# One block for the convolutions and the attention, and a single last tile

## The reference, cut to what matters

```
h = layernorm(conv2(gelu(conv1(x))) + x)            # grouped convolutions over 5 tokens, 4 hidden channels a channel
for i in range(4):                                  # linear attention with 16 heads
    q = gelu(h @ Wq[i] + bq[i]) + 0.21;  k = gelu(h @ Wk[i] + bk[i]) + 0.21;  v = h @ Wv[i] + bv[i]
    z = 1 / (q . mean(k) + 1e-6);  kv = rope(k)^T v / n
    h = layernorm((rope(q) @ kv) * z + h)
a = layernorm(gelu(h @ W1 + b1) @ W2 + b2 + h)
x = layernorm(x + a)
W1', W2' = sums over the 32 chosen of 64 low-rank pairs, with softmax weights
out = layernorm(x + gelu_tanh(x @ W1') @ W2')
```

## Time and profile before

| what | value |
|---|---|
| median of three runs | 1892.24 us |
| the profiled execution | 1893.99 us |
| its span in the trace | 1892.2 us |
| instructions | 50119 |
| TensorE busy | 1856.8 us, 98% |
| VectorE, GpSimd, ScalarE busy | 75%, 53%, 49% |
| mean granted clock of TensorE | 0.989 of full speed |

### The profile page before, as it was taken

One profiled execution on the slowest core, in us unless ns is written; L12 is line 12 of the kernel. 1 busy time (PEld: TensorE's weight loads), 2 busy tenths in 40 slices (PEclk: granted clock), 3 DMA queues, 4 the chain that ended last, 5 costly groups with the idle time before them and its releaser, 6 DMA issues.

```text
span 1892.2 us, 50119 instructions
## 1 busy us (share of the span) xinstructions
PE 1856.8 (98%) x21228; PEld 1541.2 (81%) x21228; DVE 1413.0 (75%) x3328; ACT 934.0 (49%) x1739; POOL 1011.0 (53%) x774
## 2 busy tenths in 40 slices
PE   7999899999999999999999999999999999999998
PEld 2335788888888888888887799999999999999997
DVE  2556488888888888888887767777777777777776
ACT  3544456677666766667766653232323232323231
POOL 1444699999989999999987102122222222222221
PEclk9998899999999999999999999999999999999999
DMA  7342511000101211010103850101010101101000
GB/s 266 121 172 108 198 45 37 3 35 2 36 2 37 112 46 36 2 36 2 58 2 102 306 176 12 45 23 45 24 45 27 42 31 37 41 28 45 23 12 23
DMA packets 25105, 115.63 MB, mean 61 GB/s; under 512 B 4464, under 2 KB 5040, under 8 KB 19760
## 3 DMA queue, kind: packets, MB, share of 16 engines
q1 hardware_dynamic: 19952, 85.10, 12.9%
q10 hardware_dynamic: 3776, 14.74, 2.0%
q0 software_dynamic: 1152, 12.58, 1.8%
HBM read 80.95 MB, written 31.46 MB: 59 GB/s over the span
## 4 chain that ended last, share of the span: by engine, by line
PE 86%; issue 2%; DVE 1%; ACT 1%; POOL 0%; ACTq 0%; POOLq 0%; DVEq 0%
PE bankC L34 12%; PE bankC L32 12%; PE bankC L33 12%; PE ring L32 7%; PE ring L34 6%; PE ring L33 6%; PE big L871 5%; PE big L33 3%; PE ring L808 3%; PE big L32 3%; PE big L34 3%; PE big L788 3%; PE ring L845 2%; PE ring L830 2%; PE turn L1349 1%
## 5 line engine op out<-in xcount | busy, mean ns | idle before, releaser
L32 PE MATMUL bankC<-down_hi,act_hi 128*128 128x256 f32 x1024 | 288.9, 282 | 0.0
L34 PE MATMUL bankC<-down_hi,act_lo 128*128 128x256 f32 x1024 | 286.5, 280 | 0.0
L33 PE MATMUL bankC<-down_lo,act_hi 128*128 128x256 f32 x1024 | 286.1, 279 | 0.0
L1476 DVE TENSOR_TENSOR act_lo<-gel,act_hi 128x512 fp32r<-128x512 f32 x256 | 210.6, 823 | 8.8
L34 PE MATMUL bankC<-aT_hi,up_lo 128*128 128x512 f32 x512 | 202.6, 396 | 0.0
L33 PE MATMUL bankC<-aT_lo,up_hi 128*128 128x512 f32 x512 | 202.3, 395 | 0.0
L32 PE MATMUL bankC<-aT_hi,up_hi 128*128 128x512 f32 x512 | 202.2, 395 | 0.0
L1438 POOL TENSOR_TENSOR rstdC<-var_epsC,minus_halfC 128x4 f32<-128x4 f32 x48 | 53.6, 1117 | 277.0 <-DVE var_epsC L1501 277.0
L1432 POOL TENSOR_TENSOR hC<-hC,vecC 128x1024 f32<-128x1024 f32 x16 | 38.8, 2425 | 290.5 <-PE turn L1349 290.5
L33 PEld LDWEIGHTS bankC<-down_lo,act_hi 128*128 128x128 f32 x1024 | 192.3, 188 | 1.6
L32 PEld LDWEIGHTS bankC<-down_hi,act_hi 128*128 128x128 f32 x1024 | 192.2, 188 | 1.5
(11 more groups left out here) (193 smaller groups left out, 5284.1 us busy)
## 6 DMA issues: line engine op xcount, KB each, us to landing
raw_late<-in_AB SPq DMA_DIRECT2D x30, 320.0 KB, 4.0
xs<-in_x_conv SPq DMA_DIRECT2D x16, 513.0 KB, 7.0
u<-hA SPq DMA_DIRECT2D x8, 1024.0 KB, 4.6
u_next<-u SPq DMA_DIRECT2D x8, 1024.0 KB, 4.9
hC<-u SPq DMA_DIRECT2D x16, 512.0 KB, 4.0
xC<-in_x SPq DMA_DIRECT2D x16, 512.0 KB, 4.8
out<-w_flat SPq DMA_DIRECT2D x16, 512.0 KB, 2.7
w_flat<-in_AB SPq DMA_DIRECT2D x22, 320.0 KB, 3.9
```

Of the source, the lines that this page charges most:

```text
L32: e.matmul(out, wh, xh, start=start, stop=False)
L33: e.matmul(out, wh, xl, start=False, stop=False)
L34: return e.matmul(out, wl, xh, start=False, stop=stop)
L1476: e.tensor_tensor(a_lo[:, fb, :], g, a_hi[:, fb, :].bitcast(F32), ALU.subtract).then_inc(s_act_lo, 1)
```

## The change

There is one block. The program of each engine in attention begins with that of the convolutions (`conv.sync`, `conv.gpsimd` and so on), and all buffers of both are placed by one plan of overlays.

- The first turn and split of unit 0 (`first`) are done inside the last step of the convolutions; on TensorE they and `prep.tensor` stand ahead of the last `to_tokens`.
- The q and k biases are computed as rows (the shifts, 32 equal columns, are the stationary operand; 512 columns of weights move), copied by ScalarE, and turned into columns by four matmuls with the identity.
- Tables, masks, gains and shifts are loaded by SyncE beside the convolutions (after the store of pair 1; those of q when pair 2 is through); `w_second` is loaded by GpSimd after the last split weights are stored. ScalarE's wait for those stores is gone.
- The last pair's measuring, inverting, normalising and storing (`last`) is spread over units 0 to 2 of attention.
- The ring of unit 0 waits for what the convolutions read last; `zero` is cleared after attention, since it lies over attention's masks.
- The last product of the feed-forward does its first four blocks for all tiles and then, tile by tile, the other four; tiles 0 to 2 are measured and stored together, and tile 3 by itself.

```
 def prep.tensor(e):                      # in place of lines 518 to 536
+        for cb in range(CB):
+            for l in range(L):
+                e.wait_ge(self.d_raw[l], 16)
+                m = e.matmul(self.rows_ps[32 * l:32 * l + 32, :], self.shift[:, l * CB + cb, :], self.raw[:, l, cb, 0:2 * H],
+                             start=cb == 0, stop=cb == CB - 1)
+        m.then_inc(self.s_bias, 1)
...
+    def tensor_columns(self, e, identity):
+        L = self.L
+        e.wait_ge(self.s_v, 1)
+        for k in range(2 * self.CB):
+            m = e.matmul(self.cols_ps[:, k * L:(k + 1) * L], self.rows[:, k * P:(k + 1) * P], identity[:, 0:P:P // L],
+                         start=True, stop=True)
+        m.then_inc(self.s_bias, 1)
...
+    def scalar_rows(self, e):
+        e.wait_ge(self.s_bias, 1)
+        e.activation(self.rows[:, :], self.rows_ps[:, :], ACT.Copy).then_inc(self.s_v, 1)
...
             for n in range(STEPS + LAG):             # conv_phase, tensor
                 if n < STEPS:
                     conv1(n)
+                if n == STEPS + LAG - 1:
+
+                    w.wait_ge(s_hidden, ROWS * STEPS)
+                    first()
+                    prep.tensor(e)
                 if 0 <= n - LAG < STEPS:
                     to_tokens(n - LAG)
...
-            w.wait_ge(s_convT, STEPS)
-            prep.tensor(e)
+            prep.tensor_columns(e, identity)
...
+                if q == PAIRS - 2:                   # conv_phase, sync, ahead of store(q)
+
+                    w.wait_ge(s_convT, CP * (PAIRS - 1))
+                    load_tables_q(e)
                 store(q)
...
+                if q == 1:
+                    load_tables(e)
...
+        free = {"hidden": [(s_conv, STEPS)], "ring": [(prep.s_v, 2), (prep.s_v, 2), (s_convT, STEPS), (s_y, STEPS)],
+                "biases": [(prep.s_v, 3)]}
...
+                if n == 0:                           # attention_phase, vector, ahead of rotate_k(n, 0)
+                    conv.last.vector(e, w, 0)
+                    conv.last.vector(e, w, 1)
                 rotate_k(n, 0)
                 k_mean(n)
                 for u in range(1, DUOS):
+                    if n == 0:
+                        conv.last.vector(e, w, u + 1)
                     rotate_k(n, u)
...
+                if n == 0:
+                    for half_group in range(5, 2 * conv.last.groups):
+                        conv.last.vector(e, w, half_group)
                 rotate_q(n)
...
+                if n in (1, 2):                      # attention_phase, scalar, ahead of k_mean(n)
+                    for g in (2 * n - 2, 2 * n - 1):
+                        conv.last.scalar(e, w, g)
                 k_mean(n)
...
+                else:                                # attention_phase, gpsimd, after residual(n), n < 2
+                    for g in (2 * n, 2 * n + 1):
+                        conv.last.gpsimd(e, w, g)
...
+            def last_product(i, k, s):               # ffn_phase, tensor
+
+                a_hi, a_lo = act[s]
+                order = ([(fb, t) for fb in range(FB // 2) for t in range(TILES)] +
+                         [(fb, t) for t in range(TILES) for fb in range(FB // 2, FB)])
...
+            def last_tiles(i, s, eps):               # ffn_phase, vector, in place of evict, measure, apply
+                ...
+                for a, b in (ALL_BUT_LAST, LAST):
+                    for t in range(a, b):
+                        w.wait_ge(s_down, tile_no(i, 1, s, t) + 1)
+                        e.tensor_tensor(y[s][:, t, :], bank_of(i, 1, s, FB + t)[:, 0:H], x1[s][:, t, :], ALU.add).then_inc(s_y, 1)
+                        w.wait_ge(s_y, tile_no(i, 1, s, t) + 1)
+                        e.bn_stats(stats[:, s, t, :], y[s][:, t, :]).then_inc(s_stats, 1)
+                        w.wait_ge(s_stats, TILES * n + t + 1)
+                        e.bn_aggr(moments[:, s, t, :], stats[:, s, t, :]).then_inc(s_mom, 1)
+                    w.wait_ge(s_mom, TILES * n + b)
+                    e.tensor_scalar(var_eps[:, s, a:b], moments[:, s, a:b, 1], eps, None, ALU.add).then_inc(s_var, 1)
+                for k, (a, b) in enumerate((ALL_BUT_LAST, LAST)):
+                    w.wait_ge(s_rstd, n + 1 + k)
+                    for t in range(a, b):
+                        e.tensor_scalar(y[s][:, t, :], y[s][:, t, :], moments[:, s, t, 0:1], rstd[:, s, t:t + 1], ALU.subtract,
+                                        ALU.mult).then_inc(s_ln3, 1)
```

More of the change, by code:

```diff
@@ L195, in gpsimd, with tensor @@
                     if layer == 0:
[L196 to L202, removed]
+                        prep.gpsimd_load(e, 0, keep["w_first"], keep["d_w"][0])
+                    if layer == prep.L - 1:
+                        prep.gpsimd_load(e, 1, keep["w_second"], keep["d_w"][1])
         def token_tile(q, g, s):
             return y[q % 2][:, g, :, :].rearrange("p a (j s c) -> p (a j) s c", j=ROWS, s=S)[:, :, s, :]
-        def tensor(e):
+        def tensor(e, first):
             w = Waits(e)
@@ L682, in store @@
                 e.dma_start(rows_of(u_out, b), y_of(n)[:, :, :]).then_inc(d_sent[b % 2], 16)
-            for dst, name in ((gain, "gain_rows"), (shift, "shift_rows")):
-                e.dma_start(flat(dst), tables[name].partition_broadcast(P)).then_inc(d_rows, 16)
+            conv.sync(e)
             load_u(1)
@@ L1117, in finish @@
                     step(n, i)
[L1119 removed]
+            conv.vector(e, lambda: split_u(0, 0))
+            wait_free(w, conv.free["biases"])
             for n in range(UNITS):
@@ L1625, in gpsimd @@
         def gpsimd(e, last):
+            last(0)
+            wait_free(Waits(e), before.free["ring"])
             e.memset(zero[:, :].bitcast(F32), 0.0).then_inc(s_zero, 1)
-            for g in range(2):
-                last(g)
+            last(1)
         def tensor(e, last, rows):
@@ L1782, in build @@
-        place["b1s"], place["vecC"] = sb("b1s", [P, t["b1"].shape[1]]), sb("vecC", [P, t["rows2"].shape[1]])
-        d_consts = ctx.enter_context(nc.semaphore("d_consts"))
-        d_u4 = [ctx.enter_context(nc.semaphore(f"d_u4_{s}")) for s in range(2)]
-        late = place["raw_late"]
+        u_next = sb("u_next", [P, TILES, H])
+        width = comp["AB1"].shape[2]
+        rows, split_rows, weights = [P, TILES, H], [P, CB, T], [P, 2, CB, 3 * H]
+        place = {}
+        under = lambda stack, *uses: overlay(nc, stack, place, [[(n, s, *(d or [F32])) for n, s, *d in use] for use in uses])
@@ new lines, in build @@
+        under(layers, [("hidden", [P, 2, 4, 2, T // 4 + 1])], [("gT", split_rows), ("v", [P, TILES, 8, 33])])
+        under(layers, [("w_parts", weights, F32R)], [("w_second", weights, F32R)])
+        under(layers, [("gain", [P, L, H]), ("shift", [P, L, H])])
+        under(layers, Rank.buffers(comp["logits"].shape[1] // 2, K), [("hA", [P, 2 * TILES, H])])
+        d_u0, d_u4 = [sem(f"d_u0_{b}") for b in range(2)], [sem(f"d_u4_{s}") for s in range(2)]
+        d_consts, d_early = sem("d_consts"), [sem(f"d_early{j}") for j in range(6)]
```

366 lines of the change are left out of this document (196 added, 170 removed).

## The result

The changed kernel takes 1881.46 us (median of 4 runs, 1877.92 to 1882.27) against 1892.97 us for the kernel before (1892.04 to 1894.04): 11.5 us less, ratio 0.9935, 95% interval 0.9918 to 0.9953. I had forecast 1874.0 and a range of 1871.5 to 1879. The sign was right; 7 of the 18 us are missing. The profiled execution took 1877.92 us and has no stretch at half clock while TensorE works, so it is the most favourable of the four.

The account below looks back on a forecast made before the run. TensorE, busy for 98% of the span, bounds the kernel; time can come only from its standstills or half clock. 18.8 - 2.9 = 15.9, plus 2.4, gives 18.3 us off 1892.24: 1874.0 us, range 1871.5 to 1879.

Parts of the forecast that it names:

- Hand-over until the keys are turned: From the last convolution product to unit 0's turning of the keys, which was to start 18.8 us earlier.
- Stall of VectorE: In unit 0, measuring pair 3 between key rotations delays q1 to q3: 2.9 us lost, bounds 0 and 9.6.
- Rival B: VectorE is the new bound, more measuring in the path: 9.6 instead of 2.9 us lost, 1880.6 us; chance 0.09.
- Moved at no cost: ScalarE's normalisations, GpSimd's inversions, table loads and w_second's load move into other waits: cost 0, at most 1 us.
- The clock, 0: In the hand-over and unit 0 the clock may fall, 1.7 or 2.4 us per fall; the sum takes 0.
- rival A: The clock falls once or twice in the hand-over or unit 0: 1875.7 to 1878.8 us; chance 0.28.
- The end, 2.4 us: At the kernel's end, the last store is issued 2.2 us earlier and its landing gains 0.2: 2.4 us.
- Rival C: The gain at the end doesn't appear, as the second store lands with the first's delay: 1876 us; chance 0.08.

Follow-up runs that it names:

- e6: e1 with VectorE measuring pair 3 after unit 0's four key rotations instead of between them, and GpSimd inverting after its sums: 1870.60 us.
- e1: The changed kernel with `bands_end` at 128 bytes, 96 unused bytes more ahead of down weights, up weights and w_second: 1870.49 us, ratio 0.9880.
- e3: The changed kernel with `bands_end` at 64 bytes and 64 bytes ahead of `u_next`; nearly all operands start at multiples of 128: 1875.62 us.
- e5: e1 with 64 bytes ahead of w_first and 64 behind it: 1861.62 us, ratio 0.9842.
- e10: e1 with 64 bytes behind w_first alone: 1864.45 us, ratio 0.9864.
- e7: e1 with the last product, evictions, normalisation and store as before the change: 1871.84 us.
- e8: e1 with the q and k biases again as one-column products, in their new place: 1882.74 us.
- e4: The kernel before with 32 bytes ahead of the buffers that the change had moved, nothing else: 1898.08 us, ratio 1.0028.
- e11: e5 with GpSimd's residual of unit 0 moved behind the inversions, the sums of K and the rotations of Q: 1879.03 us.

## Why the prediction was wrong

- *Hand-over until the keys are turned, 18.8 us:* right. From the end of the last convolution product it took 13.3 us, forecast 13.9, against 32.7 before.
- *Stall of VectorE, 2.9 us:* right (q3 opens 9.1 us after the turning, forecast 9.1), and e6 shows that it belongs to VectorE's queue. Rival B (9.6 us) falls; that its 1880.6 lies near the measured time is chance.
- *Moved at no cost:* right for ScalarE, GpSimd and the tables; ScalarE has 0.85 us left ahead of gelu_q. (There are sixteen normalisations, eight in each of the two units, not eight.)
- *The clock, 0:* right in the profile after (1.00 from 164 to 206 us). e1 to e3, e5 and e10 have no fall there either; e7, with the same hand-over as e1, has one of 3.4 us in unit 0 (from 186 us), and e6 the one in unit 1. So rival A can happen, and for the unprofiled runs of after it can't be excluded; it isn't what took the 9 us in the profiled one. I had the trigger right for the wrong place: in e8 the clock fell during one-column products, and in after it stayed up through waits of up to 0.9 us. The Trainium skill's idle rule (TensorE: Matmul & The Clock Gate, "The HAM clock gate"), which I weighed, would not have foreseen e8's fall, with TensorE busy throughout.
- *The end, 2.4 us:* right, 2.5 in the profiles and 2.45 between e1 and e7. From VectorE's last operation to the end of the span it took 2.94 us against 3.15, so the last landing gained the 0.2 us of the sum; the 0.9 that the prediction sets beside it, for a store alone, did not come. Rival C falls.
- *The step that failed* is one that I never priced: "I am wrong if ... later units have a pitch other than before" stands under what would show me wrong, but in the sum everything after unit 1 was taken as unchanged. The diff puts all buffers into one plan, and I read that as a question of which buffer waits for which, not of where each starts. It costs 6.6 us in the feed-forward and 2.4 in attention; e1 takes them away, and e4 brings 7.0 us of them about by itself. None of my rivals had it, so the range, 7.5 us wide, had no room for it either. Without it the sum holds: 18.8 us for hand-over and end, where 18.3 were forecast.
- *The sum for e1*, with the down weights placed as before: hand-over and end 18.8 us, less 2.2 for its longer unit 0 (35.6 against 33.4), plus 4.4 for w_second's new distance (attention units 26.05 before, 25.91 in e1, 31 of them), so 21.0; 22.1 were measured. The last microsecond is within what the clock does elsewhere. That w_second came to lie better than before (4.4 us) was luck of the padding, and not foreseen.

## What to carry to other kernels

A change of the memory plan moves every buffer behind it; before costing such a change, list the start addresses of the operands of the dominant products, before and after. For back-to-back products with 256 moving f32 columns here, a distance of 192 bytes modulo 256 between moving and stationary operand was best and 64 next. The places alone, from the changed kernel to e5, bought 10.2 us in attention's units and 8.7 in the feed-forward, as much as the whole change of schedule (18.8). Before moving an operation down a queue, look for whose buffer it is the last reader of (e11: 15 us). Read the later units' pitch too, and not only the place that was edited.

## What the hardware showed that I had not expected

- The start of an SBUF operand changes TensorE's rate: 12.27 against 12.06 us for 96 products, 5.63 against 5.35 for 48, with equal instructions and no wait. With 512 moving columns the effect is smaller: 5.47 against 5.36 us for 24 products with w_second. The up products took 0.2332 to 0.2334 us each everywhere, but their operands never changed their distance, so they show nothing on this.
- The granted clock fell during gapless one-column products (e8, 171 us), and stayed up through a hand-over with five waits of 0.4 to 0.9 us (after). After one wait of 3.9 us it was down (e6, 201 us).
- A VectorE operation on 128x4 elements took up to 2.39 us in place of 0.17 beside GpSimd's 128x1024 ones.
